# Storing a graph's edge counts with the two halves of a chunk side by side: rows of 1792 B in the loads, rows of 896 B in the stores

## The reference, cut to what matters

```python
agg = segment_sum(h[src], dst)                        # layer 0, scaled by degrees
e = exp(logits - m[dst]); out = segment_sum(e / denom[dst] * h[src], dst)
                                                      # layer 1 (two such passes), layer 2 (one)
agg = segment_sum(cat[x_dst, x_src, ea] @ W + b, dst) # layer 3, two such passes, then log_softmax
```

## Time and profile before

| what | us |
|---|---|
| median of 3 runs (4360.3 to 4362.8) | 4360.68 |
| the profiled execution | 4360.62 |
| its span | 4358.7 |
| PE busy, share of the span | 3758.0 (86%) |
| DVE busy | 3402.4 (78%) |
| ACT busy | 2873.0 (66%) |

### The profile page before, as it was taken

How to read it: one execution, slowest core, us unless ns; L and a number is a source line. 1 busy time by engine, 2 the same in 40 slices (tenths; PEclk the granted TensorE clock), 3 DMA queues, 4 the chain that set the end, 5 groups by cost and what they waited for, 6 DMA issues and landing times. The chain is left out here.

```text
span 4358.7 us, 66635 instructions
## 1 busy us (share of the span) xinstructions
PE 3758.0 (86%) x19965; PEld 2021.6 (46%) x19966; DVE 3402.4 (78%) x5051; ACT 2873.0 (66%) x3222; POOL 512.5 (12%) x1356
## 2 busy tenths in 40 slices
PE   3569999999983999899779999996999988899988
PEld 3546766666751333333433333333333333355687
DVE  9988888988966999997699999968999997711121
ACT  2046766766753999999589999985999998500001
POOL 0035555555500000000000000000000000000000
PEclk9989999999986999999989999997999999999999
DMA  2023443443447544444155544442455443378799
GB/s 70 0 70 122 141 149 127 149 140 123 157 160 105 164 161 155 155 159 122 67 166 165 164 155 155 150 131 96 157 166 163 157 155 119 112 241 247 235 336 299
DMA packets 625108, 661.04 MB, mean 152 GB/s; under 512 B 147959, under 2 KB 590585, under 8 KB 617466
## 3 DMA queue, kind: packets, MB, share of 16 engines
q1 hardware_dynamic: 604344, 524.06, 40.5%
q10 hardware_dynamic: 20548, 134.07, 7.6%
HBM read 520.69 MB, written 137.34 MB: 151 GB/s over the span
## 5 line engine op out<-in xcount | busy, mean ns | idle before, releaser
L1915 PE MATMUL psum<-sb_arena 128*65 128x448 f32 x4116 | 1729.8, 542 | 188.6 <-DVE sb_arena L1441 175.7
L1441 DVE SCALAR_TENSOR_TENSOR sb_arena<-sb_arena 128x896 f32<-128x896 f32 x1029 | 1071.3, 1087 | 208.1 <-ACT sb_arena L2331 191.2
L2323 ACT ACTIVATE psum<-sb_arena,sb_sj 128x896 f32 (+1 forms) x1029 | 1041.0, 1012 | 218.1 <-PE psum L1893 95.4
L2331 ACT ACTIVATE sb_arena<-psum,sb_sj 128x896 f32<-128x896 f32 x1029 | 1019.6, 991 | 97.6 <-PE psum L1926 97.0
L1406 DVE CUSTOM_DVE_ANT_0 sb_arena<-sb_arena 128x6272 uint8<-128x6272 uint8 (+2 forms) x189 | 990.5, 5241 | 72.0 <-DMA sb_arena<-linked 31.9
L1915 PEld LDWEIGHTS psum<-sb_arena 128*65 128x65 f32 x4116 | 557.1, 138 | 880.7 <-issue 501.6
L959 DVE TENSOR_SCALAR sb_arena<-sb_arena 128x392 f16<-128x392 f16 x2352 | 649.9, 343 | 0.0
L1926 PE MATMUL psum<-sb_arena,sb_ones 128*128 128x448 bf16 x2058 | 567.0, 358 | 46.5 <-ACT sb_arena L2300 25.4
L2148 ACT ACTIVATE sb_arena<-psum 128x784 f16<-128x784 f32 x392 | 322.7, 823 | 280.4 <-PE psum L1702 276.9
L1702 PE MATMUL psum<-sb_arena 128*128 128x392 f16 x2352 | 472.9, 337 | 40.0 <-DVE sb_arena L959 29.6
L1926 PEld LDWEIGHTS psum<-sb_arena,sb_ones 128*128 128x128 bf16 x2058 | 186.0, 97 | 600.0 <-issue 388.8
(11 more groups left out here) (294 smaller groups left out, 2289.2 us busy)
## 6 DMA issues: line engine op xcount, KB each, us to landing
sb_arena<-counts SPq DMA_DIRECT2D x490, 784.0 KB, 6.6
sb_arena<-linked SPq DMA_DIRECT2D x147, 784.0 KB, 7.7
counts<-sb_arena ACTq DMA_DIRECT2D x56, 1344.0 KB, 4.8
linked<-sb_arena ACTq DMA_DIRECT2D x60, 784.0 KB, 3.4
sb_arena<-records SPq DMA_DIRECT2D x784, 6.0 KB, 1.8
counts<-sb_arena ACTq DMA_DIRECT2D x1, 5488.0 KB, 16.4
records<-sb_arena SPq DMA_DIRECT2D x1, 3124.0 KB, 8.9
counts<-sb_arena ACTq DMA_DIRECT2D x14, 112.0 KB, 1.7
```

The lines of the kernel that those rows point to most:

```text
L1441: nc.vector.scalar_tensor_tensor(YE[:, r % RING, :], YE[:, r % RING, :], 1.0, counts_of(g, j), ALU.min, ALU.mult).then_inc(p_ready, 1)
L1915: last = nc.tensor.matmul(psum[0:D + 1, t, 0:HALF], HF[:, r * (D + 1):(r + 1) * (D + 1)], YE[:, r % RING, t * HALF:(t + 1) * HALF], start= ...
L2323: nc.scalar.activation(stage_of(odd, r), of.rearrange("p (t d) -> p t d", t=2), ACT.Relu, bias=sj8[:, r:r + 1], scale=1.0 - SLOPE).then_in ...
L2331: nc.scalar.activation(YE[:, r % RING, :].rearrange("p (t d) -> p t d", t=2), stage_of(odd, r), ACT.Exp, bias=sj2[:, r:r + 1]).then_inc(e_ ...
```

## The change

The DRAM layout of `counts` becomes `[b][a][half][d]`: for one source node all 15 halves lie behind one another, 15 x 896 B = 13,440 B, and the two halves of a chunk are one run of 1792 B. The next partition begins 49 x 13,440 = 658,560 B on.

- A load of a group is again two DMAs, now cut by blocks (3 and 4 of the 7) in place of halves, each row 1792 B. The place in SBUF and the increments are the same. So a group goes from 2 x 896 rows of 896 B to 384 + 512 rows of 1792 B.
- A piece's store takes the same bytes at the same place in the order; its run in DRAM goes from 12 blocks in one (10,752 B) to 12 rows of 896 B. The last half's store goes from 128 runs of 43,904 B to 6272 rows of 896 B.
- The path for unsorted edges changes in the same manner and does not run.

No instruction on PE, DVE, ACT or POOL is added or removed, and no wait.

```diff
-        counts = nc.dram_tensor("counts", (NH + 1, BLK, NB, HALF), fp16, kind="Internal").ap()
+        counts = nc.dram_tensor("counts", (BLK, NB, NH + 1, HALF), fp16, kind="Internal").ap()
...
             sp.wait_ge(cnt_free, c * NGRP + (L * ROWS // GRP + CS + 1 + before))
-            to = cnt[:, g % CS, :].rearrange("p (a t d) -> p a t d", a=GRP, t=2)
-            for t in range(2):
-                of = counts[c * 2 + (t + 1):c * 2 + (t + 2)] if isinstance(c, int) else counts[bass.ds(c * 2 + (t + 1), 1)]
-                sp.dma_start(to[:, :, t, :], of[:, :, g * GRP:(g + 1) * GRP, :].rearrange("o b a d -> b (o a) d")
-                             ).then_inc(cnt_in[g], 16)
+            of = counts[:, :, c * 2 + 1:c * 2 + 3, :] if isinstance(c, int) else counts[:, :, bass.ds(c * 2 + 1, 2), :]
+            for a0, a1 in ((0, GRP // 2), (GRP // 2, GRP)):
+                sp.dma_start(cnt[:, g % CS, a0 * CW:a1 * CW].rearrange("p (a n) -> p a n", n=CW),
+                             of[:, g * GRP + a0:g * GRP + a1].rearrange("b a t d -> b a (t d)")).then_inc(cnt_in[g], 16)
...
-            PIECE = NB // 4 * HALF
+            PIECE = NB // 4
...
-                    n0, n1 = p * PIECE, (p + 1) * PIECE if p < 4 else NB * HALF
-                    act.dma_start(counts[bass.ds(h, 1)].rearrange("o b a d -> b (o a d)")[:, n0:n1], stage[:, slot, n0:n1]).then_inc(counts_stored, 16)
+                    a0, a1 = p * PIECE, (p + 1) * PIECE if p < 4 else NB
+                    act.dma_start(counts[:, a0:a1, bass.ds(h, 1), :].rearrange("b a o d -> b a (o d)"),
+                                  stage[:, slot, a0 * HALF:a1 * HALF].rearrange("p (a d) -> p a d", d=HALF)).then_inc(counts_stored, 16)
...
-                act.dma_start(counts[NH].rearrange("b a d -> b (a d)"), stage[:, (NH - 1) % 2, :]).then_inc(counts_stored, 16)
+                act.dma_start(counts[:, :, NH, :], stage[:, (NH - 1) % 2, :].rearrange("p (a d) -> p a d", a=NB)).then_inc(counts_stored, 16)
```

More of the change, by code:

```diff
@@ L554, in _ @@
                     sp.wait_ge(stage_ready, h + 2)
-                    sp.dma_start(counts[bass.ds(h + 1, 1)].rearrange("o b a d -> b (o a d)"),
-                                 ap1(stage[:, bass.ds(h % 2, 1), :])).then_inc(counts_out, 16)
+                    sp.dma_start(counts[:, :, bass.ds(h + 1, 1), :].rearrange("b a o d -> b a (o d)"),
+                                 ap1(stage[:, bass.ds(h % 2, 1), :]).rearrange("p (a d) -> p a d", a=NB)).then_inc(counts_out, 16)
                     with sp.Fori(0, 2) as pair:
```

## The result

The kernel after takes 4351.17 us (median of 11 runs, 4346.17 to 4358.49), the kernel before, beside it on the same chip, 4360.49 us (11 runs). The ratio is 0.9979, 95% interval 0.9969 to 0.9988: 9.3 us faster, 5 to 14 us by the interval. The direction is as forecast and the time lies in the range, but the gain is less than half of the forecast's 20.1 us.

A forecast was written before the change was run, and what follows sets the result against it. PE was taken to bound all but the second pass of layer 3, which went at the loads' pace. Second pass -20.1, start of layer 3 -0.5, last store +0.5 us: 4340.5 us from 4360.62, range 4335 to 4358.

The forecast's parts named there:

- What bounds the kernel: Whole kernel: PE bounds build, attention and first pass; faster loads help only the second pass and one first load.
- Second pass: Layer 3, second pass: 38 groups at 4.22 us instead of 4.749, 20.1 us less; bounds 0 and 21.6 us.
- the slots then fill ahead of it: Second pass: once the DMA wait goes, PE's own 49 matmuls a group are late and loads run ahead.
- The 381 GB/s: Second-pass loads: rate for 1792 B rows, from a fixed part plus a part per byte fitted through 896 and 6272 B rows.
- Start of layer 3: First group's load before PE starts: 4.22 us instead of 4.75, so 0.5 us less.
- The issues on ACT: Build: 56 big pieces issue 0.04 to 0.08 us longer each; taken as 0, upper end 5 us.
- The pieces' landing: Build: a big piece lands in about 6 us in place of 4.8, covered by 30 us; cost 0.
- The last half's store: End of build, line 2166: 6272 rows in one DMA may hold ACT's next issue; 0.5 us more, ends 0 and 9.
- The sum: Whole kernel: -20.1 - 0.5 + 0.5 = -20.1 us against 4360.62 us, forecast 4340.5 us.
- rival (a): Second pass: gain there but small, 355 GB/s, 4.52 us a group, 8.7 us less, 4352 us; chance 0.16.
- (b): Second-pass loads: scatter in DRAM takes what longer rows give, 338 GB/s again, 4360.5 us; chance 0.12.
- (c): Second pass: scattered reads 658,560 B apart are slower; at 300 GB/s 23 us are added, 4384 us; chance 0.12.

The follow-up runs named there:

- rows_of_6272: Kernel before with each SBUF slot laid out as [half][node][448], so each half loads in contiguous rows of 6272 B: 4342.95 us, ratio 0.9943.
- after_best: Kernel after with `cnt` shifted 184 B in SBUF onto a multiple of 256 B and the last half stored in five pieces: 4342.75 us, ratio 0.9948.
- before_on_256: Kernel before with one line added, shifting `cnt` by 184 B in SBUF onto a multiple of 256 B: 4341.88 us, ratio 0.9946.
- pieces_issued_twice: Kernel before with each piece's store issued as two DMAs of half its columns, 70 more issues on ACT: 4366.54 us, ratio 1.0001.
- old_loads_new_stores: Stores of the kernel after with the loads of the kernel before, so the layers work on other values: 4368.62 us, ratio 1.0009.
- short_rows_by_node: Kernel after's DRAM layout and stores, but loaded by halves in rows of 896 B, 13,440 B apart: 4369.88 us, ratio 1.0012.
- rows_on_1792: Kernel after with a DRAM pitch of 16 halves per node instead of 15, so rows start at multiples of 1792 B: ratio 0.9976.
- the traces with pieces: Kernel after with the last half stored in five pieces, not one DMA: 4352.9 and 4350.2 us; also that plus a 184 B SBUF shift, 4342.75 us.

## Why the prediction was right in sign and too high in gain

**What bounds the kernel**: right. Attention (2519.0 for 2518.7 us) and the first pass (327.7 for 327.8) did not move, and but for half a microsecond at the start of layer 3 all the gain is in the second pass.

**Second pass: the term was mis-sized, 13 us instead of 20.1.** The step that failed is "38 x (4.749 - 4.22)": that every group would come at the pace of the rate. The pace itself is right, 4.21 us as a median. But in the mean a group takes 172.6 us / 39 = 4.43, since eight come late: 38 x (4.749 - 4.43) = 12 us, 13.3 by the length of the pass. The error in thought was that "the slots then fill ahead of it". At 381 GB/s the loads take 4.22 us and PE 4.18, so the slots never fill, and PE waits for what comes late: 7.7 us in 8. rows_of_6272 (215.6 us) and after_best (214.7), with loads at about 400 GB/s and more, have more late groups (14 and 10 intervals over 0.45 us above the median) and yet keep what I forecast, with 3.5 us of waits each. The rate is not the whole account, though: before_on_256, at the pace of the kernel after, has only four late groups and a pass of 218.2 us. What makes a group late, and why fewer are in that kernel, is not shown.

**The 381 GB/s were right by accident.** I fit a fixed part and a part per byte through 896 B and 6272 B rows. The mechanism is another: blocks of 256 B touched in SBUF. Before, two rows for a node touch 4 + 5 = 9 blocks, after 8, and 9 / 8 x 338 = 380. By the fit, before_on_256 would have gained nothing; it gained 22 us. The 3 cycles a packet of the Trainium skill (DMA: Bandwidth & Descriptors, Why small descriptors are slow), which I weighed against the fit, gave 5%; the DMA views show 338 and, where nothing is late, about 381 GB/s, 13% more, and the same for rows of 896 B that only lie better (before_on_256).

**Start of layer 3**: forecast -0.5 us, measured 10.9 to 10.4 us of PE's wait (the earlier trace rows and the tile's view above). Right.

**The issues on ACT**: 0 was right within what the times can tell, by pieces_issued_twice. SP's came out 37 ns shorter instead of equal, and nobody waits for them.

**The pieces' landing**: forecast 6 us, measured 5.7; cost 0, and new stores leave the long stretch of the build within its drift.

**The last half's store**: mis-sized, +0.5 us forecast, +3.3 measured, and +3.4 to +6.4 in other traces with the same store. I took the hold to end when half of the store has landed, 9.5 us behind the issue (half of 18.6 is 9.3), and ACT's next DMA to come 9.4 us behind; by that the term would have been 0.1 us or nothing, and the 0.5 had no row behind it. It came 11.3 us behind and was still held to 14.1 (in old_loads_new_stores from 9.7 to 15.4); the landing takes 20.1 us, so the hold lasts to about 0.70 to 0.77 of it. The measured cost lies within the stated ends, 0 and 9 us.

**The sum**: -13.3 - 0.5 + 3.3 to 6.4 makes 7.4 to 10.5 us less; measured 9.3. The range held. The rival (a) names nearly this time, 4352 us, by a rate of 355 GB/s. The mean of the pass was near that, 362, but by another way: the median group came at 381 GB/s, and eight came late. Rivals (b) and (c) fall by short_rows_by_node: 338 GB/s with rows scattered over 658,560 B of pitch. The loss that the Trainium skill (DMA: Bandwidth & Descriptors, Latency and other measured facts) reports for row pitches at large powers of two does not show itself at this pitch, which is none, nor at the 702,464 B of rows_on_1792 (222.7 us).

**What stays open**: what makes groups late, and why the kernel before, with the same 16 KB packets of instructions, has two late intervals (5.6 and 6.0 us) and not eight; the stretch between build and layer 3 in the traces with pieces; the cap at 404 GB/s.

## What to carry to other kernels

Before the layout in DRAM is changed for faster loads, look where the tile lies in SBUF: the price of a row went by the blocks of 256 B that it touches there, and 184 B of padding gave 22 us where the new layout gave 9 and, in its second run, 14. Where loads and an engine need nearly the same time, the sum by means is too good: ask how much faster than the engine the loads are, since what lands late is then waited for. Behind a store of 6272 rows in one DMA, ACT's next DMA took 2.8 and 5.7 us to issue in place of 0.36; behind five pieces it was hardly held.

## What the runs showed that I had not expected

Two loads of the same bytes, rows and source ran at 375 and 309 GB/s, by 128 B in SBUF (2.14 and 2.60 us for 784 KB). DRAM starts and pitches, on the other hand, changed nothing that the landings could show. Beside fetches of code, 16 KB on one of 16 engines for 0.9 to 1.5 us, groups landed up to 1.7 us late, eight times in the kernel after and twice in the kernel before. And the alternation stood in the DMA view of the kernel before all along, at slices of 0.5 us; over 181 us it is averaged to a smooth 337 GB/s.
